# A four-layer graph network on one core: the first layer's edge store, loads and vector steps in another order

## The reference

```python
diff = e[:, :, :, None] - offsets                 # 64 Gaussian centres, e = A = adj
g = jnp.exp(coeff * diff * diff)
h = ssp(jnp.einsum('bijg,fg->bijf', g, W1) + b1)  # ssp(x) = softplus(x) - ln 2
Wf = jnp.einsum('bijf,gf->bijg', h, W2) + b2
rf = jnp.einsum('bjd,fd->bjf', r, Wa)
Wf = Wf * Am                                      # Am = A[..., None]
y = jnp.einsum('bjf,bijf->bif', rf, Wf * Am)
y = ssp(jnp.einsum('bif,df->bid', y, Wd1) + bd1)
y = jnp.einsum('bid,ed->bie', y, Wd2) + bd2
x = _layernorm(x + y, axis=-1)
```

## Time and profile before

| | us |
|---|---|
| median of 3 runs | 1793.87 (1790.25 to 1794.85) |
| profiled execution, its own time | 1793.05 |
| its span, first to last instruction | 1791.5 |
| PE busy | 1315.6 (73%) |
| DVE busy | 1149.4 (64%) |
| POOL busy | 836.4 (47%) |
| ACT busy | 799.8 (45%) |
| DMA queue of SP, share of 16 engines | 25.7% of the span |
| mean granted clock of TensorE | 0.835 |

### The profile page before, as it was taken

The page is one execution under the profiler, slowest core; times in us unless marked ns, Lnnn a source line. Parts: engine busy times, 40 slices in busy tenths (PEclk is TensorE's granted clock), DMA queues, the critical chain, the costliest instruction groups (busy, mean ns, idle before and its releaser), DMA issues. The chain is left out here.

```text
span 1791.5 us, 30457 instructions
## 1 busy us (share of the span) xinstructions
PE 1315.6 (73%) x6048; PEld 875.4 (49%) x6048; DVE 1149.4 (64%) x4287; ACT 799.8 (45%) x2049; POOL 836.4 (47%) x1314
## 2 busy tenths in 40 slices
PE   3787777878877777777745665665775888888994
PEld 2444444444544444444423554554654555555774
DVE  4776776776776667677636888888886233333227
ACT  2655565565555655565532222322331233333237
POOL 4655565665665556565633566565564000000006
PEclk9888888898798889888876777878778899999558
DMA  3544454455344544444410000000000000000003
GB/s 88 141 131 123 134 141 122 125 139 134 118 129 126 137 127 123 131 136 126 124 44 18 13 24 12 23 23 12 24 24 7 1 0 0 0 0 0 0 1 95
DMA packets 148630, 128.89 MB, mean 72 GB/s; under 512 B 64963, under 2 KB 127839, under 8 KB 148577
## 3 DMA queue, kind: packets, MB, share of 16 engines
q1 hardware_dynamic: 146852, 127.20, 25.7%
q10 hardware_dynamic: 1725, 1.13, 0.2%
HBM read 123.05 MB, written 5.21 MB: 72 GB/s over the span
## 5 line engine op out<-in xcount | busy, mean ns | idle before, releaser
L542 POOL TENSOR_TENSOR sum<-msg 128x384 f32<-128x384 f32 (+1 forms) x128 | 143.1, 1118 | 299.5 <-DVE msg L922 299.5
L750 PE MATMUL wf<-hid,w2t 128*128 128x384 f32 x512 | 256.9, 635 | 2.0 <-DVE msg L922 2.0
L922 DVE SCALAR_TENSOR_TENSOR msg<-wf,b2c,rv 128x768 f32<-128x768 f32 x128 | 130.0, 1016 | 149.5 <-PE wf L750 142.9
L750 PEld LDWEIGHTS wf<-hid,w2t 128*128 128x128 f32 x512 | 108.5, 235 | 141.7 <-issue 117.5
L1653 POOL MEMSET r_minus_half<- 128x4 f32 x1 | 0.1, 102 | 351.0 <-POOLq L1523 351.0
L651 ACT ACTIVATE dist<-val_bc,noff_c 128x384 f32<-128x384 f32 x128 | 79.2, 619 | 154.6 <-DMA val_bc<-edge_val 154.6
L742 PE MATMUL zb<-gauss,w1t 64*128 64x384 f32 x256 | 144.9, 653 | 2.9 <-ACT expd L662 2.9
L743 PE MATMUL zb<-gauss,w1t 64*128 64x384 f32 x256 | 145.0, 653 | 0.0
L662 ACT ACTIVATE expd<-zb,safe_b,reached 128x768 f32<-128x768 f32 x128 | 125.8, 983 | 42.0 <-PE zb L743 41.5
L1601 DVE SCALAR_TENSOR_TENSOR r_new<-r_gates 128x64 f32<-128x64 f32 x128 | 28.9, 225 | 165.7 <-ACT r_gates L1582 165.7
L1549 PEld LDWEIGHTS r_zgi<-xin,w_hh 128*128 128x128 f32 x508 | 78.4, 215 | 91.3 <-issue 81.8
(11 more groups left out here) (276 smaller groups left out, 3804.1 us busy)
## 6 DMA issues: line engine op xcount, KB each, us to landing
sq_bc<-edge_sq SPq DMA_DIRECT2D x128, 384.0 KB, 4.7
val_bc<-edge_val SPq DMA_DIRECT2D x256, 96.0 KB, 2.7
idx_bc<-edge_idx SPq DMA_DIRECT2D x128, 192.0 KB, 3.5
adj_w<-in_adj_rows SPq DMA_DIRECT2D x64, 64.0 KB, 2.8
xt_w<-in_x_cols SPq DMA_DIRECT2D x64, 64.0 KB, 2.5
xin<-in_x_rows SPq DMA_DIRECT2D x32, 128.0 KB, 2.4
m_adj_g<-in_adj_rows SPq DMA_DIRECT2D x16, 256.0 KB, 2.7
m_adjt_g<-in_adj_t SPq DMA_DIRECT2D x16, 256.0 KB, 2.7
```

The source lines that it names most:

```text
L542: pool.tensor_tensor(sum1[:, 0:wide, :], m[:, 0:wide, :], m[:, wide:2 * wide, :], ALU.add)\
L750: last = pe.matmul(wf[:, half, 0:HALF], w2t[:, :], hid[:, q, half * HALF:(half + 1) * HALF], start=True, stop=True)
L922: dve.scalar_tensor_tensor(halves(msg[:, q, :]), wf[:, :, 0:HALF], b2c[:, :], halves(rv[:, i % 2, :]), ALU.add, ALU.mult)\
```

## The change

1. SP stores the edges of g+2 first in its even unit, ahead of the other loads. It waits for their landing where it did.
2. val_bc, idx_bc and sq_bc are loaded for both units of a graph by one DMA each (two for val_bc, one per half). Their semaphores are those of the even buffer of the pair (loaded()).
3. squares is made by ScalarE, ahead of ei; one semaphore, edges16, covers both. GpSimd no longer copies the last rank: over_cnt has a column per graph, and the check at the end reads that.
4. VectorE computes t_h (decoder's maximum) ahead of the ranking.
5. slot_from and over_t are written as a compare times a tensor of ones.

The dense fallback, run only if a graph has too many edges, keeps its loads.

```diff
+            def load_graph(u, d, g, dg):
+                q = u.mod(UNIT_BUFS, d)
+                after(sp, "dist2_ready", u, d + 1 - UNIT_BUFS, u0)
+                after(sp, "pick_ready", u, d + 1 - UNIT_BUFS, u0)
...
+                for half in range(2):
+                    part = slice(half * NG, (half + 1) * NG)
+                    sp.dma_start(val_bc[part, q:q + 2, :], edge_val[gi, :, part, :].rearrange("a k i r -> a k (i r)")
+                                 .broadcast_to((NG, 2, HALF))).then_inc(val_in[q], 16)
+                sp.dma_start(idx_bc[:, q:q + 2, :], edge_idx[gi, :, :, :].rearrange("a k i r -> a k (i r)")
+                             .broadcast_to((P, 2, UNIT))).then_inc(unit_in[q], 16)
+            def load_squares_of_graph(u, d, g, dg):
...
+                after_parity(sp, "rv_even", u, d - UNIT_BUFS)
+                after_parity(sp, "rv_odd", u, d + 1 - UNIT_BUFS)
+                sp.dma_start(sq_bc[:, q:q + 2, :], edge_sq[bass.ds(g.at(dg), 1), :, :, :]
+                             .rearrange("a k i r -> a k (i r)").broadcast_to((P, 2, UNIT))).then_inc(sq_in[q], 16)
...
+                    if not dense and i % 2 == 0 and g.has(2):
+                        w(sp, "edges16", g.at(2) + 1)
...
+                            sp.dma_start(dst[bass.ds(g.at(2), 1), :, :, :].rearrange("a h i r -> (a i) h r"),
+                                         src.rearrange("p (h r) -> p h r", h=2)).then_inc(edges_stored, 16)
                     if i % per_graph == 0:
...
                     if not dense and i % 2 == 0 and g.has(1):
-                        for kk in range(2):
-                            load_squares(u, 2 + kk, g, 1, kk)
+                        load_squares_of_graph(u, 2, g, 1)
                     if not dense and i % 2 == 0 and g.has(2):
-                        w(sp, "edges16", g.at(2) + 1)
-                        w(sp, "squares_ready", g.at(2) + 1)
...
                         sp.wait_ge(edges_stored, 48 * (g.at(2) + 1))
-                        for kk in range(2):
-                            load_unit(u, 4 + kk, g, 2, kk)
+                        load_graph(u, 4, g, 2)
...
-                        pool.tensor_copy(last_rank[:, bass.ds(g.at(2), 1)], found[:, q, RANKS - 1:RANKS])
-                        pool.tensor_tensor(squares[:, q, :], found[:, q, 0:2 * R], found[:, q, 0:2 * R], ALU.mult)\
-                            .then_inc(s["squares_ready"], 1)
...
+                        act.activation(squares[:, q, :], found[:, q, 0:2 * R], ACT.Square)
                         act.activation(ei16[:, q, :], found[:, q, RANKS:RANKS + 2 * R], ACT.Copy)\
                             .then_inc(s["edges16"], 1)
...
-                dve.tensor_scalar(slot_from[:, :], iota_row[:, :], start, None, ALU.is_ge)
+                dve.scalar_tensor_tensor(slot_from[:, :], iota_row[:, :], start, k["ones"][:, :], ALU.is_ge, ALU.mult)
...
-                    if not dense and k_in == 0 and g.has(3):
-                        rank_edges(g)
                     if k_in == 0 and g.has(-2):
                         w(dve, "ulog_ready", g.at(-2) + g0 + 1)
                         dve.scalar_tensor_tensor(t_h[:, :], p_u, bd1c[:, :], t_lg[:, :], ALU.add, ALU.max)\
                             .then_inc(s["uh_ready"], 1)
+                    if not dense and k_in == 0 and g.has(3):
+                        rank_edges(g)
...
-                        dve.tensor_scalar(over_t[:, g.mod(2), :], iota_row[:, :], over_row[:, bass.ds(g.at(), 1)], None,
-                                          ALU.is_equal).then_inc(s["over_t_ready"], 1)
+                        dve.scalar_tensor_tensor(over_t[:, g.mod(2), :], iota_row[:, :], over_row[:, bass.ds(g.at(), 1)],
+                                                 k["ones"][:, :], ALU.is_equal, ALU.mult).then_inc(s["over_t_ready"], 1)
```

More of the change, by code:

```diff
@@ L237, in layer0 @@
     over_bits = sb("over_bits", [P, OVER])
-    over_cnt = sb("over_cnt", [P, 1])
+    over_cnt = sb("over_cnt", [P, B])
     slot_from = sb("slot_from", [P, P])
@@ L311, in layer0 @@
         "top1 top2 top3 rest1 rest2 idx3 idxf cnt start_ready start_copied from_ready slot_ready over_gathered "
-        "hits_ready picks_ready edges16 squares_ready adj_read least_ready "
+        "hits_ready picks_ready edges16 adj_read least_ready "
         "dist2_ready gauss_ready z_ready abs_ready relu_ready exp_ready log_ready hid_ready pick_ready valsq_ready "
@@ L354, in graph, with loaded, unit_count @@
             return Steps(pair, i // per_graph, 2, ng)
-        def unit_count(u, d, each=16):
-            before_pair = per_pair // UNIT_BUFS
-            return u.pair * (each * before_pair) + each * ((u.inner + d) // UNIT_BUFS + 1 + u0 // UNIT_BUFS)
+        def loaded(u, d):
+            q = u.mod(UNIT_BUFS, d)
+            return q if dense else q // 2 * 2
+        def unit_count(u, d, each):
+            earlier = u0 // UNIT_BUFS if loaded(u, d) % 2 == 0 else 0
+            return u.pair * (each * (per_pair // UNIT_BUFS)) + each * ((u.inner + d) // UNIT_BUFS + 1 + earlier)
         def adj_count(g, q, d=0):
@@ L434, in body @@
                     u, g = unit(pair, i), graph(pair, i)
+                    if not dense and i % 2 == 0 and g.has(2):
+                        w(sp, "edges16", g.at(2) + 1)
+                        alone(sp)
+                        q = g.mod(2, 2)
+                        for dst, src in ((edge_val, found[:, q, 0:2 * R]), (edge_sq, squares[:, q, :]),
+                                         (edge_idx, ei16[:, q, :])):
+                            sp.dma_start(dst[bass.ds(g.at(2), 1), :, :, :].rearrange("a h i r -> (a i) h r"),
+                                         src.rearrange("p (h r) -> p h r", h=2)).then_inc(edges_stored, 16)
                     if i % per_graph == 0:
@@ L507, in body @@
                     k_in = i % per_graph
[L508 to L513, removed]
-                        pool.tensor_copy(last_rank[:, bass.ds(g.at(2), 1)], found[:, q, RANKS - 1:RANKS])
-                        pool.tensor_tensor(squares[:, q, :], found[:, q, 0:2 * R], found[:, q, 0:2 * R], ALU.mult)\
-                            .then_inc(s["squares_ready"], 1)
                     if dense and u.has(1):
                         q = u.mod(UNIT_BUFS, 1)
-                        pool.wait_ge(sq_in[q], unit_count(u, 1, 16))
+                        pool.wait_ge(sq_in[loaded(u, 1)], unit_count(u, 1, 16))
                         pool.tensor_tensor(sq_bc[:, q, :], sq_bc[:, q, :], sq_bc[:, q, :], ALU.mult)\
@@ L731, in body @@
                             w(pe, "rfhi_ready", g.at(1) + 1)
-                        pe.matmul(p_start, before[:, :], over_cnt[:, :], start=True, stop=True)\
+                        pe.matmul(p_start, before[:, :], over_cnt[:, bass.ds(g.at(3), 1)], start=True, stop=True)\
                             .then_inc(s["start_ready"], 1)
@@ L854, in place_overflow @@
                 w(dve, "cnt", n)
-                dve.tensor_scalar(slot_from[:, :], iota_row[:, :], start, None, ALU.is_ge)
-                dve.tensor_tensor(over_end[:, bass.ds(g.at(3), 1)], start, over_cnt[:, :], ALU.add)\
+                dve.scalar_tensor_tensor(slot_from[:, :], iota_row[:, :], start, k["ones"][:, :], ALU.is_ge, ALU.mult)
+                dve.tensor_tensor(over_end[:, bass.ds(g.at(3), 1)], start, over_cnt[:, bass.ds(g.at(3), 1)], ALU.add)\
                     .then_inc(s["from_ready"], 1)
@@ L960, in _ @@
             dve.tensor_scalar(bad[:, 0, :], over_end[:, :], float(P), None, ALU.is_gt)
-            dve.tensor_scalar(bad[:, 1, :], last_rank[:, :], 0.0, None, ALU.is_gt)
+            dve.tensor_scalar(bad[:, 1, :], over_cnt[:, :], OVER - 0.5, None, ALU.is_gt)
             dve.tensor_scalar(bad[:, 2, :], least[:, :], 0.0, None, ALU.is_gt)
```

24 lines of the change are left out of this document (12 added, 12 removed).

## The result

The changed kernel takes 1670.15 us (median of 4 runs, 1662.28 to 1696.98) against 1794.36 us before (1790.25 to 1813.34 in 4). The ratio is 0.930, with a 95% interval of 0.921 to 0.939. The forecast was 1669. On a second chip the same two kernels took 1702.2 and 1809.2 us: 0.938, interval 0.930 to 0.945. The profiled execution shown here took 1696.98 us, the longest of the four.

The account below looks back on a forecast made before the run. SP's DMA queue was taken to bound the first layer at 13.73 us a graph; a new path of 11.5 + 0.15 + 0.1 = 11.75 gains 1.98 x63 = 125 us, from 1793.87 to 1669 us, range 1632 to 1735.

Parts of the forecast that it names:

- SP's queue was the period: First layer, SP's DMA queue: 8.4 us of issue work and a 5.2 us landing make the 13.73 us a graph.
- The new path by rfe, t_lg, t_h, ranking, msg, rf_lo: Closed path across engines in the first layer, claimed to bind next at 11.5 us; VectorE waits about 0.8 for t_lg.
- the sum: The added pieces of the path from one rfe to the next in the first layer: 11.5 us a graph.
- the allowances: Added to 11.5 us: 0.15 for meetings of VectorE and GpSimd, 0.1 for clock falls, giving 11.75 a graph.
- the move: On VectorE, t_h ahead of the ranking makes the ranking wait; without it 10.6 to 11.0 us a graph was expected.
- The 0.1 us for a semaphore: Piece of the path between t_lg's end and t_h on VectorE, priced at 0.1 us.
- The landing of the merged loads: On SP's queue, data 10.6 to 12.6 us after rfe, against 13.2 when needed: hidden, 0.6 to 2.6 us to spare.
- The clock: TensorE's granted clock, 0.85 before, was to be 0.95 or more in 100:750; 0.1 us a graph allowed for falls.
- The compares: slot_of's two-tensor form given to over_t and slot_from on VectorE: priced at 0, over_t still 0.7 to 0.9 us.
- The other small edits: Squares and the last rank's copy leave GpSimd, off the binding path; over_cnt as a column per graph costs nothing.
- 13.73 - 11.75: First layer's period before less the forecast period: a gain of 1.98 us a graph, x63 = 125 us.
- The landing still binds: Rival: stores and merged loads queue so long that time stays at 1790 to 1797 us; chance 0.03.

Follow-up runs that it names:

- loads for each unit: The changed kernel with one set of loads for each unit again, stores still first: 1650.04 us, ratio 0.929, period 11.79 us.
- the second run: The changed kernel run again with no edit, on another chip: 1702.20 us, ratio 0.938, period 12.36 us.
- the compares back: The changed kernel with a set of loads for each unit, and slot_from and over_t again as tensor_scalar: 1658.52 us, ratio 0.927, period 11.72 us.
- stores first: The kernel before with the three stores moved to the head of SP's even unit, nothing else: 1677.54 us, ratio 0.931, period 11.82 us.
- small edits: The changed kernel with a set of loads for each unit and the ranking again ahead of t_h: 1636.15 us, ratio 0.918, period 11.49 us.
- t_h first: The changed kernel with a set of loads for each unit, t_h still ahead of the ranking: 1650.04 us, ratio 0.929, period 11.79 us.
- merged loads: The changed kernel itself, with one load for both units: 1670.15 us, ratio 0.930, period 12.11 us in its first profile.
- SP's part alone: The kernel before with only the stores put first on SP and the loads merged for both units: 1735.91 us, ratio 0.956, period 13.14 us.
- the one with the ranking first: The changed kernel with the ranking again ahead of t_h: 1688.40 us, ratio 0.933, period 12.36 us.
- the one with squares on GpSimd: The changed kernel with squares made on GpSimd again and SP also waiting for squares_ready: 1687.13 us, ratio 0.951, period 12.33 us.

## Why the prediction was right, point by point

- **SP's queue was the period: right, and shown.** Moving its stores alone gives 0.931; taking away TensorE's wait for t_h alone gives 1.000. SP's wait for the landing fell from 4.9 to 2.1 us a graph, as forecast (about 2), and it stands idle ahead of the stores, 3.4 us.
- **The new path by rfe, t_lg, t_h, ranking, msg, rf_lo: right, but not alone.** VectorE waits 0.77 us for t_lg (0.8 forecast), TensorE's wait for t_h is gone. With loads for each unit the path shows openly at 11.79 us, where the sum had 11.5 and the allowances made it 11.75. Undoing the move there gains 0.3 us, not the 0.5 to 0.9 that the forecast put on it (11.5 against 10.6 to 11.0): the values' wait came back (26.7 us over 57 graphs) and so did TensorE's for t_h. The 0.1 us for a semaphore had no row behind it; the profile after has 0.03 from t_lg to t_h.
- **The landing of the merged loads: wrong.** The step that failed inside a forecast that held is "2.7 for such a load now; if it queues behind the squares, 4.7", with "0.6 to 2.6 us to spare". The rows show a median of 5.1 us for the values, and in the graph of the second run 5.75 us from the end of issue (411.62) to the distances (417.37). The stores' landing was priced too short as well: 4.15 in the sum, and 4.79 and 4.78 us from the end of their issue to the next loads in the two graphs shown (407.36 to 412.15 and 405.41 to 410.19). So 0.70 us a graph of waiting remained. The sentence "Fewer, larger DMAs carry the same bytes" priced the merge at nothing. It costs 1.3 us a graph in the kernel before with the stores first (13.14 against 11.82, 0.956 against 0.931). In the changed kernel it is 0.3 to 0.6 by the periods (12.11 and 12.36 against 11.79), on different chips and not apart by the ratios.
- **The clock: nearly.** 0.93 instead of 0.95 or more. With loads for each unit, where ScalarE hardly waits for the values, it is 0.95 and 0.96 (the compares back), which fits falls that follow that wait.
- **The compares: right.** Priced at 0, measured at 0, at a small loss per instruction.
- **The other small edits: wrong where the landing leaves room.** The forecast had them "off the path above" at no price. Squares on ScalarE and the copy that is gone give about 0.3 us a graph with the stores first and loads for each unit. One edit after another, the periods read 11.82 (stores first), 11.49 (small edits), 11.79 (t_h first), 12.11 (merged loads): what the small edits gave, the move of t_h took back, and by these periods the merge cost as much again. These are single executions on three chips, so the last step is the least sure.
- **The size.** The layer gained 102 us by the first profile (12.11) and 86 by the second (12.36), where the sum had 125. That the median came out 1 us from 1669 is luck. The time behind the layer varies by some 20 us and more from one execution to the next; the profile of before had 889 us of it, where seven others have 865.5 to 869.2. With 39.5 + 763 us to the last rfe, 866 us behind it and 2 around the span, the median of 1670 is met, so the missing 22 us probably come from a stretch that the change does not touch (those executions were not profiled). The mechanism was right in the main, and the term that was too large is 13.73 - 11.75: it should have been 1.4 to 1.6.
- **The rivals.** "The landing still binds" had 0.03, for its pure form. A half form of it, in which the landing binds along with the path, fits what happened.

What stays open: why SP's part alone is as slow as 13.14 us, while two kernels with the same loads reach the changed kernel's level: the one with the ranking first (12.36, which adds the new place of squares) and the one with squares on GpSimd (12.33, which adds that of t_h). Both also have what those two do not differ in: no copy of the last rank ahead of squares, a column per graph in over_cnt, and the compares with ones. That common part is the simplest candidate, and no run tests it on its own. SP's wait for squares does not tell them apart: 189.5 us over 48 graphs in the slow one, 216.5 over 53 with squares on GpSimd.

## What to carry to other kernels

Before pricing an engine's waits, look for a queue whose round closes exactly on the period; here a DMA queue in which stores stood behind loads that nobody needed yet. Merging DMAs saves issue time, and it makes the consumer of the first part wait until the whole load has landed; here, with the queue's order put right, it gained nothing and cost up to 1.3 us a graph, so test the two apart. When one bound goes, size at least the next two, with landings taken under the new order of the queue and not the old one.

## What the runs showed of the hardware

- The DMA engines were busy for longer per byte where the broadcast of the squares was issued while the small stores ahead of it had not landed. With the stores at the head of the queue and the squares behind them (three small loads between), the engines' share was 0.62 for 146 GB/s (merged) and 0.66 for 151 (for each unit). Before, with the squares ahead of the stores, it was 0.48 for 130. With the squares issued after the stores' landing, behind the values, it was 0.54 for 150, and the squares landed in 5.7 us instead of 7.6. Why is not shown.

```profile
sq_bc<-edge_sq SPq DMA_DIRECT2D x54, 768.0 KB, 5.7
val_bc<-edge_val SPq DMA_DIRECT2D x108, 192.0 KB, 3.5
```

- The stores of 6 KB and less, in pieces of 24 bytes and 12, land 4.7 us after their issue in the changed kernel (the last of the three, median), with little ahead of them, and 5.4 behind the loads before. The lowest median in any run that has one is 4.3 us, so their place in the queue is worth more than their size suggests.
- The stretch behind the first layer took 865.5 to 924.4 us in the profiled executions of unchanged code, at a mean granted clock of TensorE between 0.86 and 0.76: 865.5 to 869.2 us at 0.85 to 0.86, 889 to 893 at 0.81 to 0.82, 908 at 0.79, 924 at 0.76. A difference of 1% between two kernels is read from the layer that was changed, not from the total.
